# Adding gathered node rows onto edge attributes inside the transfer, in layer two of a two-layer graph network

## The reference

```
h = relu(layernorm(x));  x = x + ci * segment_sum((h * cj)[src], dst)
h = relu(layernorm(x));  x = x + (1 + eps) * h + segment_sum(relu(h[src] + edge_attr), dst)
```

## Time and profile before

| | |
|---|---|
| median of three runs, not profiled | 4982.61 us |
| span of the profiled execution | 8580.9 us |
| busy in that span: PE, DVE, ACT, POOL | 4359.2, 3658.4, 3124.7, 3610.0 us |
| indirect gathers of layer two | 1250 |
| VectorE additions `plain_sum` | 50 |

### The profile page before, as it was taken

One profiled execution on the slowest core, in us unless ns is written; L12 is line 12 of the kernel. 1 busy time (PEld: TensorE's weight loads), 2 busy tenths in 40 slices (PEclk: granted clock), 3 DMA queues, 4 the chain that ended last, 5 costly groups with the idle time before them and its releaser, 6 DMA issues.

```text
span 8580.9 us, 129759 instructions
## 1 busy us (share of the span) xinstructions
PE 4359.2 (51%) x44428; PEld 3164.9 (37%) x44428; DVE 3658.4 (43%) x11303; ACT 3124.7 (36%) x8299; POOL 3610.0 (42%) x3712
## 2 busy tenths in 40 slices
PE   0555555555555555555555555445444444545444
PEld 0333333333333333333333333334334343434343
DVE  6444444444444444444444444434343333434334
ACT  0333434343333333333333333234333333433333
POOL 7444444444444444444444444343443434343442
PEclk8777777777777777777777777666666666666666
DMA  5111111111111111111111100101110111101110
GB/s 90 31 31 31 31 31 31 31 30 31 30 31 30 31 30 31 30 31 30 31 30 31 31 17 17 43 22 31 30 32 22 32 29 32 31 22 32 30 32 17
DMA packets 437255, 265.45 MB, mean 31 GB/s; under 512 B 330740, under 2 KB 421220, under 8 KB 430120
## 3 DMA queue, kind: packets, MB, share of 16 engines
q1 hardware_dynamic: 318264, 185.91, 9.1%
q0 software_dynamic: 116960, 65.42, 4.4%
q10 hardware_dynamic: 1296, 4.79, 0.2%
HBM read 176.35 MB, written 79.52 MB: 30 GB/s over the span
## 4 chain that ended last, share of the span: by engine, by line
PE 36%; issue 26%; another core or an unknown queue 22%; DVE 9%; ACT 5%; SPq 1%; DVEq 0%; ACTq 0%; DMA 0%; POOL 0%; POOLq 0%
PE candidates L1179 16%; DVE arena L1663 5%; PE candidates L1105 5%; PE plain_ps L1191 4%; PE sorted_agg L1122 4%; DVE arena L1639 3%; PE key_rows L1074 2%; ACT centered L974 2%; PE candidates L1100 2%; ACT message L920 2%; PE plain_ps L1143 1%; PE candidates L1092 1%; ACT arena L821 1%; PE plain_ps L1151 1%
## 5 line engine op out<-in xcount | busy, mean ns | idle before, releaser
L710 POOL DMA_INDIRECT records<-stage,place_i x1875 | 1821.1, 971 | 675.8 <-issue 625.1
L698 POOL DMA_INDIRECT stage<-table,src_plain x1250 | 1193.9, 955 | 1778.1 <-DMA stage<-in_edge_attr 1386.7
L1639 DVE TENSOR_SCALAR arena<-arena,row_key 125x1280 bf16<-125x1280 f16 x1000 | 552.6, 553 | 2554.9 <-ACT arena L821 1776.0
L920 ACT ACTIVATE message<-candidates,member_is 128x96 bf16<-128x96 f32 x3600 | 912.4, 352 | 1643.5 <-remote 922.8
L691 POOL DMA_INDIRECT message<-table,mid_src x480 | 533.5, 1112 | 2234.8 <-PE plain_ps L1151 2095.5
L1105 PE MATMUL candidates<-parts,arena 125*128 125x32 bf16 x15000 | 589.2, 181 | 1214.2 <-issue 1211.8
L821 ACT ACTIVATE arena<-key_rows 125x640 f16<-125x640 f16 x1000 | 662.5, 719 | 1237.3 <-remote 987.2
L1663 DVE TENSOR_SCALAR arena<-window_iota,dst_rel 128x224 bf16<-128x224 f16 (+1 forms) x4800 | 1025.9, 280 | 112.4 <-remote 67.7
L1105 PEld LDWEIGHTS candidates<-parts,arena 125*128 125x128 bf16 x15000 | 503.7, 99 | 1384.6 <-issue 1370.1
L1092 PE MATMUL candidates<-parts,arena 125*128 125x96 bf16 x5000 | 312.0, 220 | 1312.9 <-ACT message L920 748.6
L1074 PE MATMUL key_rows<-ident,record 128*125 128x128 f16 x5000 | 494.6, 242 | 878.4 <-issue 587.7
(11 more groups left out here) (224 smaller groups left out, 5798.9 us busy)
## 6 DMA issues: line engine op xcount, KB each, us to landing
record<-records SPq DMA_DIRECT2D x50, 1650.0 KB, 7.1
stage<-in_edge_attr SPq DMA_DIRECT2D x125, 400.0 KB, 3.2
records<-pad SPq DMA_DIRECT2D x25, 1650.0 KB, 10.7
records<-stage,place_i POOLq DMA_INDIRECT x1875
stage<-table,src_plain POOLq DMA_INDIRECT x1250
message<-table,mid_src POOLq DMA_INDIRECT x480
xs<-in_x SPq DMA_DIRECT2D x8, 390.6 KB
table<-parts ACTq DMA_DIRECT2D x4, 585.9 KB
```

The source lines that it names most:

```text
L698: pool.indirect_dma_start(message[:, k, j, :] if l == 0 else rows[:, k, j, :], None, table0 if l == 0 else table1, bass.IndirectOffsetOnAx ...
L710: pool.indirect_dma_start(records, bass.IndirectOffsetOnAxis(ap=place_i[:, h, e:e + 1], axis=0), stage[:, h, e, :], None).then_inc(scatter ...
L920: last = nc.scalar.activation(direct_message[n % DB][:, m * WIDE:(m + 1) * WIDE], candidates[n % 2][:, m * WIDE:(m + 1) * WIDE], ACT.Copy, ...
L1639: nc.vector.tensor_scalar(src_onehot[:, g % 2, o, :], key_row[:, g % 2, :], row_key[0:NP, o:o + 1], None, ALU.is_equal).then_inc(src_oneho ...
```

## The change

The gathers of layer two get `attr` as destination and an operation: `compute_op=ALU.add` makes the transfer add each node row onto what lies in SBUF. VectorE's addition, its semaphore and the buffer `rows` go. GpSimd no longer waits for `plain_sum_ready`. ScalarE's relu waits for the 25 gathers themselves. Layer one's gathers keep `bypass`, a plain copy. The path for far edges changes in the same way; no edge of these inputs takes it.

```diff
-        rows = room[:, 0:PLAIN * J * F].rearrange("p (k j f) -> p k j f", k=PLAIN, j=J)
-        attr = room[:, PLAIN * J * F:2 * PLAIN * J * F].rearrange("p (k j f) -> p k j f", k=PLAIN, j=J)
+        attr = room[:, 0:PLAIN * J * F].rearrange("p (k j f) -> p k j f", k=PLAIN, j=J)
...
-                        message[:, k, j, :] if l == 0 else rows[:, k, j, :], None, table0 if l == 0 else table1,
-                        bass.IndirectOffsetOnAxis(ap=indices[:, j:j + 1], axis=0)).then_inc(landed, 16)
+                        message[:, k, j, :] if l == 0 else attr[:, k, j, :], None, table0 if l == 0 else table1,
+                        bass.IndirectOffsetOnAxis(ap=indices[:, j:j + 1], axis=0),
+                        compute_op=ALU.bypass if l == 0 else ALU.add).then_inc(landed, 16)
...
                     pool.wait_ge(plain_loaded[k], 32 * (b + 1))
-
-                    at_least(pool, plain_sum_ready, 2 * b - 1 + k if not is_first(b) else 0)
                     gather(1, k, range(J), gathered[1][k], src_plain[:, k, 0:J])
...
-                        act.wait_ge(plain_sum_ready, 2 * b + k + 1)
+                        act.wait_ge(gathered[1][k], 16 * J * (b + 1))
...
-                    def plain_sum(k):
-                        dve.wait_ge(gathered[1][k], 16 * J * (b + 1))
-                        dve.wait_ge(plain_loaded[k], 32 * (b + 1))
-                        nc.vector.tensor_tensor(attr[:, k, :, :], attr[:, k, :, :], rows[:, k, :, :], ALU.add).then_inc(plain_sum_ready, 1)
...
-                        if g == 0 or g == 5 and not is_last(b):
-                            plain_sum(g // 5)
...
-                        plain_sum(1)
                         plain_after_first(1)
```

More of the change, by code:

```diff
@@ L388, in gnn_two_layers @@
         plain_onehot_ready = per_layer("plain_onehot_ready")
-        plain_sum_ready = sem("plain_sum_ready")
         plain_first = sem("plain_first")
@@ L1885, in _ @@
                             dve.wait_ge(far_gathered[l], 16 * J * (s + 1))
-                            nc.vector.tensor_tensor(attr[:, 0, :, :], attr[:, 0, :, :], rows[:, 0, :, :], ALU.add).then_inc(far_sum, 1)
+                            dve.sem_inc(far_sum, 1)
                             dve.wait_ge(far_first, s + 1)
```

## The result

The changed kernel takes 5701.4 us (median of four runs, 5697.5 to 5705.41), the kernel before 4982.05 us (median of four, 4977.06 to 4985.43). The ratio is 1.1448, with a 95% interval of 1.1431 to 1.1464: 719 us slower, and 121 us beyond the upper end of the forecast range.

The account below looks back on a forecast made before the run. GpSimd's queue of transfers was taken to set the pace in both layers. To 4982.6 us came 196 us for 1250 adding gathers, less 1 us at the end: 5178 us, range 4995 to 5380 us.

Parts of the forecast that it names:

- the price of an adding gather: On GpSimd in layer two: 157 ns more for each of 1250 gathers, 196 us in total; chance 0.28.
- the three forms: GpSimd's indirect transfers in the first profile: scatter of 132-byte rows (971 ns), gathers of 128-byte (955) and 192-byte rows (1112).
- three for two: Rival: layer two's gathers priced by accesses to a row, 478 ns more each, 597 us, 5580 us; chance 0.24.
- a second transfer: Rival and upper bound: each adding gather costs 1.26 us more, 1575 us in total, 6557 us; chance 0.06.
- GpSimd's queue as the bound: Unprofiled, GpSimd's transfers set the pace in both layers: 1260 ns per gather, 31.5 us per unit in layer two.
- the rival of a VectorE-bound layer: Layer two bound by VectorE: up to 0.16 us per gather unseen, 45 us come back, 4938 us; chance 0.16.
- that of an unchanged price: Rival: adding gathers in layer two cost what copies do, so no change, 4982 us; chance 0.26.
- The crawl: TensorE's slow matmuls during layer two's bursts of gathers, 1.2 to 2.6 us of issue each, taken for the recording's load.
- VectorE's addition at nothing: Removing 50 additions in layer two gives VectorE 45 us back, but was costed at nothing for the kernel's time.
- the prediction's two reasons: VectorE waits for the relu at L1827 anyway, 2.8 us each; with GpSimd as bound, 3.7 us per unit is cover.
- The moved wait and GpSimd's dropped wait: Gathers awaited by ScalarE's group 1, not VectorE's group 0: only idle time moves; GpSimd not awaiting the addition: 0 us.
- The sign that I gave for VectorE's idle time: VectorE's wait at L1827 in layer two should grow from 2.8 to some 3.7 us per unit.

Follow-up runs that it names:

- the half rows: Changed kernel with each adding gather of layer two fetching and adding 16 of a row's 32 features; 5704.93 us.
- with `bypass`: Changed kernel with a plain copy in place of the add in layer two's gathers, attributes left out of the sum; 4957.78 us, ratio 0.9958.
- the second recording of before: The kernel before, unchanged, profiled once more; 4977.74 us, span 4975.8 us.

## Why the prediction was wrong

**The step that failed** is the price of an adding gather: "the distance between the cheapest and the dearest of the three forms, 1112 - 955 = 157 ns". It is 596 ns by medians. 1250 x 0.596 = 745 us, less the 22 us that the rest of the change gains, gives 723 us, against 719 measured. The mechanism and the sign were right (GpSimd sets the pace, so every 0.01 us of a gather is 12.5 us); the term was mis-sized by almost four.

Its source was weak in two ways. The 157 ns were a difference of one recording, gone in the next; and in the earlier trace rows itself L698 into `message` fetches the same 192-byte rows as L691, for 945 ns instead of 1112. Besides, the three rows differ in bytes and direction, of which the half rows show the bytes to cost nothing; none of them has anything to do with adding. The range failed by the same step: its upper end priced the sum by accesses, three for two, 478 ns. That rival came nearest, but what grows with the rows is only 168 of the 596 ns; the rest comes once for each gather. The Trainium skill's page "Collectives: The Full Stack", section "The bandwidth ceiling: the fold count and why AG ≠ RS ≠ AR", stood behind it, with two read descriptors for a sum. The packets agree in kind, as a sum has more of them (144 for 32), but the 0.43 us that no row brings stay where only 48 packets are left, so the packets do not explain them. The other bound, a second transfer (1.26 us), had a price of that kind, once for each gather, but was above the truth, and the row nearest to an unknown price was taken where the whole stretch between the bounds was open.

**GpSimd's queue as the bound** held: 29.1 us of waiting for transfers in layer two of the kernel before (25.4 and 3.7), and the copies of 32 rows, 69 us cheaper in GpSimd's busy time than those of 128 without the addition, made that kernel 67 us faster. With that the rival of a VectorE-bound layer falls; so does that of an unchanged price.

**The crawl** was the recording's, as argued; but only that one's. What caused it was not found.

**VectorE's addition at nothing**: its own 45 us were indeed covered, but the cost stood on another engine. It held up 28 gathers, by 19.2 us, a cost that neither of the prediction's two reasons counts. Without it the gathers were 12.8 us shorter and the end 7.3 us, where 1 us was forecast. Beside the dear gathers this doesn't show; with `bypass` it does.

**The moved wait and GpSimd's dropped wait** cost nothing, as forecast: GpSimd never waits for the relu or a load in the changed kernel. The sign that I gave for VectorE's idle time was right in direction only: its wait at the step behind the relu was to grow to 3.7 us per unit and is 1091.5 / 50 = 21.8 us, since the price was so much larger.

```profile
L1819 DVE SCALAR_TENSOR_TENSOR stage<-stage,message 128x800 f32<-128x800 f32 x50 | 49.6, 992 | 1091.5 <-ACT message L985 1091.5
```

**The DMA engines** are not in the way, as forecast: in the changed kernel GpSimd's queue holds 10.5% of them and the busiest one 14.4%.

```profile
q1 hardware_dynamic: 318264, 185.91, 14.4%
```

## What to carry to other kernels

An operation that rides on a transfer is free only if the queue that issues the transfer has time: here it moved 1 us of an engine with slack, once per unit, to 25 x 0.6 us of the engine that set the pace. Where the price of an unseen operation is multiplied by 1250, the gap between the bounds is the forecast, and a small difference between unlike rows doesn't narrow it. Before a recording is used for prices, see that its span agrees with the time of the runs.

## What the runs showed of the hardware

- An indirect gather with an addition costs GpSimd 1540 ns for 128 rows where a copy costs 944: by estimate about 430 ns more once for each transfer and 1.3 ns more for each row (from 32, 64 and 128 rows), whether a row has 64 bytes or 128.
- Its transfers are cut differently: 16 packets and one for each row, where a copy has 32 for 128, 64 or 32 rows.
- A plain adding transfer of 128 x 3200 bytes from SBUF to SBUF took GpSimd 1.01 us.
- A gather that starts while VectorE adds two operands in SBUF (at least 0.04 us behind the addition's start, with at least 0.15 us of it left) lasts longer by what is left of the addition, less 0.13 us: 28 of 28 in the second recording of before, by up to 0.82 us. L1639, with one tensor and one number for each partition, held 124 of 124. A reduction of the same length (39 starts) and an instruction with one of its two operands in PSUM (144 starts) held none.
- Fifty additions of this kind, 1 us each, lengthened GpSimd's gathers by 42.0 us in total, in part through other instructions that then met more starts.
